# Cross attention of a post-norm decoder: scores as three rounded products, a looked-up weight table decoded in 32 units instead of 64

## The chip, the cores and the metric
One core of a Trainium2 chip runs one program. The metric is the device time of one execution in microseconds. Engines are named as in the profile: PE (TensorE) with PEld (its weight loads), DVE (VectorE), ACT (ScalarE), POOL (GpSimd) and SP (SyncE, which issues most DMAs here). All times below are in us unless marked ns.

## The reference
Six stages on x (4 chunks of 512 rows, width 512), each followed by a residual sum and a layer norm: two attentions and a feed-forward of layer 0, then self attention, cross attention and feed-forward of layer 1. The change touches the cross attention and the decoding of the last feed-forward's weights:

```python
q = (hidden_states @ Wq).reshape(B, Sq, 16, 128)
k = (encoder_hidden_states @ Wk).reshape(B, Skv, 16, 128)
v = (encoder_hidden_states @ Wv).reshape(B, Skv, 16, 128)
q = rmsnorm(q, gq)
k = rmsnorm(k, gk)
scores = jnp.einsum('bqhd,bkhd->bhqk', q, k) * scale
attn = jax.nn.softmax(scores, axis=-1)
out = jnp.einsum('bhqk,bkhd->bqhd', attn, v).reshape(B, Sq, 2048) @ Wo
# next stage: three weight matrices, each w = lut[idx] with 16 table entries, 3 * 512 * 1376 indices
```

## The kernel before
**Stages.** Each stage loops over the 4 chunks c. The cross attention (stage 3 of the code, line 820 on) is written out by hand for PE, ACT, DVE, POOL and SP; every engine runs its own list, tied by semaphores. A chunk has a start (keys and values of the first four heads, x turned), 16 heads hh in four groups g of four, an output phase (16 heads against Wo) and the norms.

**PE in head hh** (lines 934 to 947): scores(hh), four tiles of 128 x 512, each a full f32 product of q4 and kr (line 905, shown as L594); queries(hh+1), 12 rounded products of 512 columns (L844); weighted(hh-1), full f32 (L594); in the second head of a group the values of the next group, 24 rounded products (L844); turn_keys(hh+1) (L890); query_squares(hh+1) (L897); turn_weights(hh) (L912); in the third head the keys of the next group, 24 rounded products. A rounded product works on fp32r operands: a number is split into its rounded part (hi, written by ACT) and the rest (lo, a subtraction on DVE), and hi*hi + hi*lo + lo*hi makes the product. queries, keys and values are made so before the change already.

**Banks.** Tiles of the list TILES4 go through three PSUM banks in turn (bank4, line 835): a tile waits until ACT has copied the tile three places before it. A query tile is followed by the output tile of head hh-1, then by value tiles or the turned keys, then by the turned weights. The scores have banks 4 to 7.

**DVE in head hh** (lines 1730 to 1758): for each of four tiles the maximum (L1734) and its scaled negative (L1738, which for the first tile waits for POOL's power of the query's mean square); then four reciprocals (L1743) and scalings (L1745) after ACT's exponentials; in the last head of a group key_scale (L1686), on which turn_keys of the next head waits; look_up(c, hh); query_mean(hh+1) (L1692); in the third head key_norms (L1675, L1677). In chunk 0 it also makes the rests of the weights (L1696, L1700, L1704), in head 12 that of the next chunk's context (L1708).

**look_up** (line 1628) decodes one of 64 units of 128 x 258 indices, one a head: four masks of index bits (L1634, L1636), eight entries of the table's pairs (L1640), seven predicated choices in three rounds of 4, 2 and 1 (L1648), each round behind one wait. All work of one unit stands together, after the softmax of its head. SP loads the indices and stores the 64 results; stage 4 reads them.

**ACT in head hh**: exponentials (L1240), squares (L1230) and copy of the next query (L1040 through bring), the copies of the output tile, of values, turned keys (turned_keys, line 1233), turned weights and keys.

**Output phase** (line 955): in chunks 0 to 2 each head takes 12 rounded products (L960 to L962). ACT rounds the head's output and its slice of Wo (round_out), DVE makes both rests (out_rest, L1717 and L1718), two buffers each; PE waits for out_rest(hh), ACT for PE to be done with head hh-2. DVE does nothing else there. The last chunk's output phase is in full f32 (L970).

## Time and profile before

| what | us |
|---|---|
| three runs | 2951.90, 2947.09, 2952.43; median 2951.9 |
| the profiled execution | 2950.78, its span 2948.8 |
| PE busy / DVE busy / ACT busy / POOL busy | 2639.7 / 2067.5 / 1178.3 / 641.9 |
| mean granted TensorE clock | 0.95 |
| cross attention, first scores of chunk 0 to first scores of chunks 1, 2, 3 | at 1262.7, 1610.3, 1928.4, 2247.7 |

The profile is one execution. Busy time is that of an engine's own instructions; matmuls overlap, so a row of several has the span of all. A number in brackets is the engine's idle time just before the instruction, and what ended it. The granted clock is the share of 2.4 GHz that TensorE was given: 1.00, or 0.50, which is 1.2 GHz.

### The profile page before, as it was taken

The numbers are of one execution on the slowest core, as the hardware profiler recorded it, in microseconds if no ns is written. First come the engines' busy times: TensorE is split into PE (matmuls) and PEld (weight loads), VectorE is DVE, ScalarE is ACT, GpSimd is POOL, SyncE is SP. The second block draws the span as 40 slices with busy tenths as digits, with TensorE's granted clock in tenths as the row PEclk, the third lists the DMA queues.
The fourth block names the chain that finished last, engine by engine and source line by source line (L and its number), as shares of the span: only waits on it lengthen the run. The fifth ranks groups of instructions, "written<-read, shape, count | busy, mean of one in ns | idle before, by whom it ended". The sixth has DMA issues, their size and how long they took to land.

```text
span 2948.8 us, 30680 instructions
## 1 busy us (share of the span) xinstructions
PE 2639.7 (90%) x9586; PEld 1640.0 (56%) x9586; DVE 2067.5 (70%) x4063; ACT 1178.3 (40%) x2139; POOL 641.9 (22%) x569
## 2 busy tenths in 40 slices
PE   6888888888869978789989999999989998999998
PEld 2333333333337844456657666666666665488886
DVE  3996996996996547778876888588867887322232
ACT  4335325326333312255554555355544555121111
POOL 0642543534520135411101111011101110000000
PEclk9998988988979999999999999999999999999999
DMA  3111111111220212233233222332222223400000
GB/s 120 57 50 44 65 43 55 61 50 51 69 109 29 79 43 86 77 122 101 86 102 116 83 83 76 92 108 83 83 74 95 83 72 107 138 1 29 29 15 14
DMA packets 90792, 212.58 MB, mean 72 GB/s; under 512 B 9987, under 2 KB 34819, under 8 KB 86534
## 3 DMA queue, kind: packets, MB, share of 16 engines
q1 hardware_dynamic: 81510, 178.51, 18.7%
q0 software_dynamic: 5472, 21.01, 1.9%
q10 hardware_dynamic: 3648, 11.08, 1.0%
q8 instruction: 80, 1.31, 0.2%
q14 instruction: 82, 0.67, 0.1%
HBM read 164.10 MB, written 46.47 MB: 71 GB/s over the span
## 4 chain that ended last, share of the span: by engine, by line
PE 59%; DVE 20%; issue 11%; POOL 5%; ACT 3%; DMA 1%; SPq 1%; DVEq 0%; POOLq 0%; ACTq 0%
PE bank L594 21%; PE bank L844 8%; PE bank L912 3%; DVE h L1441 3%; PE bank L984 3%; PE bank L985 3%; PE bank L988 3%; POOL h L1822 3%; DVE val L1640 2%; DVE sm L1734 2%; DVE val L1648 2%; PE bank L714 2%; PE bank L970 2%; PE bank L960 2%; PE bank L961 1%
## 5 line engine op out<-in xcount | busy, mean ns | idle before, releaser
L1822 POOL TENSOR_TENSOR h<-du,Bb 128x1024 f32<-128x1024 f32 x128 | 306.2, 2394 | 188.1 <-DVE h L1446 172.2
L1441 DVE TENSOR_TENSOR_SCAN h<-bank,h 128x512 f32<-128x512 f32 x256 | 297.8, 1203 | 22.4 <-POOL h L1822 15.1
L1095 ACT ACTIVATE bank<-dt,A 128x512 f32<-128x512 f32 x256 | 175.9, 691 | 327.7 <-DVE h L1441 327.6
L1240 ACT ACTIVATE p<-bank,sm,rq 128x512 f32<-128x512 f32 x256 | 199.1, 778 | 244.5 <-DVE sm L1738 244.5
L1890 POOL TENSOR_TENSOR rq<-rq,mhalf 128x4 f32<-128x4 f32 x64 | 69.4, 1084 | 798.3 <-DVE rq L1692 798.3
L594 PE MATMUL bank<-pT,v 128*128 128x512 f32 x512 | 236.7, 606 | 2.7 <-ACT pT L1040 2.7
L211 POOL TENSOR_SCALAR rstd<-mv 128x1 f32<-128x1 f32 x96 | 25.2, 263 | 956.5 <-DVE mv L205 956.5
L594 PE MATMUL bank<-kr,q 128*128 128x512 f32 x512 | 233.0, 598 | 0.0
L714 PE MATMUL bank<-h,ident 128*128 128x512 f32 x256 | 153.2, 682 | 84.6 <-DVE h L1446 84.5
L844 PE MATMUL bank<-x_hi,wxq_s 128*128 128x512 f32 x512 | 190.8, 454 | 6.5 <-DVE x_lo L1713 6.5
L1648 DVE COPY_PREDICATED val<-msk,val 128x258 f32<-128x258 int32 x448 | 173.6, 449 | 27.8 <-DVE val L1648 0.2
L1734 DVE TENSOR_REDUCE sm<-bank 128x1 f32<-128x512 f32 x256 | 175.2, 684 | 23.6 <-PE bank L594 23.6
L1777 DVE TENSOR_TENSOR h<-bank,sg 128x512 f32<-128x512 f32 (+1 forms) x44 | 30.4, 690 | 228.5 <-PE bank L988 228.5
L1446 DVE TENSOR_TENSOR h<-h,Cb 128x1024 f32<-128x1024 f32 x128 | 173.8, 1358 | 6.6
L1640 DVE TENSOR_SCALAR val<-msk,lx,le 128x258 uint32<-128x258 uint32 x512 | 171.7, 409 | 7.2 <-DVE msk L1636 0.5
L594 PEld LDWEIGHTS bank<-pT,v 128*128 128x128 f32 x512 | 99.1, 194 | 106.9 <-issue 97.6
L912 PE MATMUL bank<-ident,p 128*128 128x128 f32 x1024 | 138.9, 293 | 17.4 <-DVE p L1745 16.2
L1040 ACT ACTIVATE pT<-bank 128x512 f32<-128x512 f32 x256 | 134.7, 603 | 46.9 <-PE bank L912 46.8
L594 PEld LDWEIGHTS bank<-kr,q 128*128 128x128 f32 x512 | 94.4, 193 | 94.4 <-issue 93.4
L715 PE MATMUL bank<-h,ident 128*128 128x512 f32 x256 | 140.9, 634 | 0.0
L714 PEld LDWEIGHTS bank<-h,ident 128*128 128x128 f32 x256 | 43.6, 202 | 172.3 <-DVE h L1446 137.3
L912 PEld LDWEIGHTS bank<-ident,p 128*128 128x128 f32 x1024 | 125.6, 155 | 24.4 <-DVE p L1745 19.5
(228 smaller groups left out, 5686.4 us busy)
## 6 DMA issues: line engine op xcount, KB each, us to landing
wxq_s<-wq_dram SPq DMA_DIRECT2D x48, 512.0 KB, 4.5
Bb<-bc_dram SPq DMA_DIRECT2D x32, 512.0 KB, 3.6
Cb<-bc_dram SPq DMA_DIRECT2D x32, 512.0 KB, 3.7
x_dram<-xo POOLq DMA_DIRECT2D x16, 1024.0 KB, 4.7
xc<-x_dram SPq DMA_DIRECT2D x16, 1024.0 KB, 5.2
woh<-in_Wo SPq DMA_DIRECT2D x64, 256.0 KB, 2.7
wxv_s<-wkv_dram SPq DMA_DIRECT2D x12, 1024.0 KB, 5.3
wxk_s<-wkv_dram SPq DMA_DIRECT2D x12, 1024.0 KB, 7.4
```

The costliest lines, as they stand in the source:

```text
L594: m = pe.matmul(dst, l, r, start=(k == 0), stop=(k == len(pairs) - 1))
L714: pe.matmul(bank[4 + et][:, :], ident[:, :], h[:, U % HR, 0, :], start=(w == 0), stop=False)
L844: m = pe.matmul(dst, l, r, start=(n == 0), stop=(n == len(pairs) - 1))
L912: m = pe.transpose(d[:, t * P:(t + 1) * P], p4[:, t, k * P:(k + 1) * P], ident[:, :])
L1095: act.activation(bank[2 + n][:, :], dt[:, et, :], ACT.Exp, scale=A[:, et, 2 * w + n:2 * w + n + 1]).then_inc(dA_ready, 1)
L1240: act.activation(p4[:, t, :], bank[4 + t][:, :], ACT.Exp, bias=sm4[:, 4 + t:5 + t], scale=rq[:, hh % 2, 1, t:t + 1], accum_out=sm4[:, 8 + ...
L1441: dve.tensor_tensor_scan(h[:, s, n, :], bank[2 + n][:, :], h[:, s, n, :], 0.0, ALU.mult, ALU.add).then_inc(scanned, 1)
L1446: dve.tensor_tensor(h[:, s, :, :], h[:, s, :, :], Cb[:, w % 2, :, :], ALU.mult).then_inc(hC_ready, 1)
L1640: dve.tensor_scalar(val[:, j, :].bitcast(U32), msk[:, 0, :].bitcast(U32), lx[:, j:j + 1], le[:, j:j + 1], ALU.bitwise_and, ALU.bitwise_xor ...
L1648: dve.copy_predicated(val[:, s, :], msk[:, b, :], val[:, s + (1 << (b - 1)), :]).then_inc(lut_step, 1)
L1734: dve.tensor_reduce(sm4[:, t:t + 1], bank[4 + t][:, :], AX.X, ALU.max).then_inc(max_ready, 1)
L1822: pool.tensor_tensor(h[:, U % HR, :, :], du[:, et:et + 1, :].to_broadcast([P, 2, S]), Bb[:, w % 2, :, :], ALU.mult).then_inc(dBu_ready, 1)
```

## The change
Scores are made of q_hi, q_lo, k_hi and k_lo. ACT's copy of the query writes q_hi (fp32r) and DVE subtracts it from the bank (q_rest), so the bank is now also held until q_rest; ACT copies the turned keys to kr as before, then rounds kr to k_hi, and DVE makes k_lo (k_rest). q4 and kr had two buffers; q_hi, q_lo, k_hi, k_lo and kr have one.

The table has 32 units of 516 columns. A unit is cut into masks and four pairs, which stand in different heads; each choice waits for the instruction before it. The number of units per group of heads is LUTS; what a chunk has left of its 8 units (2, 1, 1, 0) is decoded in its output phase. In a group with two units head 0 holds masks and pairs 1 and 2 of the first, head 1 its pairs 3 and 4 and masks and pair 1 of the second, head 2 pairs 2 and 3, head 3 pair 4. Index buffers and results alternate between two places, and SP's loads and stores move with the units.

```diff
-UNITS = B * XH
+UNITS = B * XH // 2
+UB = UNITS // B
+LUTS = ((2, 1, 2, 1), (2, 2, 2, 1), (2, 2, 2, 1), (2, 2, 2, 2))
...
-        w_hi3 = Space(nc, s4.at)("w_hi3", [P, 2, D], F32R); q4 = s4("q4", [P, 2, S])
+        w_hi3 = Space(nc, s4.at)("w_hi3", [P, 2, D], F32R); q_hi = s4("q_hi", [P, S], F32R); q_lo = s4("q_lo", [P, S], F32R)
...
-        w_lo3 = Space(nc, s4.at)("w_lo3", [P, 2, D], F32R); kr = s4("kr", [P, 2, S])
+        w_lo3 = Space(nc, s4.at)("w_lo3", [P, 2, D], F32R); k_hi = s4("k_hi", [P, S], F32R); k_lo = s4("k_lo", [P, S], F32R)
+        kr = s4("kr", [P, S])
...
-        idx = s4("idx", [P, UL], I32); msk = s4("msk", [P, 4, UL], I32); val = s4("val", [P, 8, UL])
+        idx = s4("idx", [P, 2, UL], I32); msk = s4("msk", [P, 3, UL], I32); val = s4("val", [P, 5, UL])
@@ SP @@
+                def load_idx(n):
+                    if n >= 2:
+                        sp.wait_ge(lut_step, START + 19 * (n - 1))
+                    sp.dma_start(idx[:, n % 2, :], io["idx"][bass.ds(n, 1), :, :].rearrange("a p n -> p (a n)")).then_inc(idx_in[n % 2], 16)
+                def store_unit(n):
+                    sp.wait_ge(lut_step, START + 19 * (n + 1))
+                    sp.dma_start(w_dram.rearrange("(u p n) -> u p n", p=P, n=UL)[bass.ds(n, 1), :, :]
+                                 .rearrange("a p n -> p (a n)"), val[:, 4 * (n % 2), :]).then_inc(w_out[n % 2], 16)
...
+                            g, n = hh // 4, UB * c + sum(LUTS[c][:hh // 4])
+                            if hh % 4 == 0:
+                                load_idx(n)
+                                if g and LUTS[c][g - 1] == 2:
+                                    store_unit(n - 1)
+                                if LUTS[c][g] == 2:
+                                    load_idx(n + 1)
+                            if hh % 4 == 2:
+                                store_unit(n)
@@ PE @@
                             pe.wait_ge(a_done, START + A0[3] + after(c, PER_A[3], max(0, k - 2)))
+                            for hh in range(XH):
+                                if TILES4["q", hh] == k - 3:
+                                    pe.wait_ge(q_split, START + after(c, XH, hh + 1))
...
-                            ready4("kT", hh)
+                            pe.wait_ge(q_split, START + after(c, XH, hh + 1))
+                            pe.wait_ge(k_split, START + after(c, XH, hh + 1))
...
-                                group(bank[4 + t][:, :], [(q4[:, hh % 2, t * P:(t + 1) * P], kr[:, hh % 2, :])], v_full)
+                                tt = slice(t * P, (t + 1) * P)
+                                three4(bank[4 + t][:, :], [(q_hi[:, tt], k_hi[:, :]), (q_hi[:, tt], k_lo[:, :]), (q_lo[:, tt], k_hi[:, :])], v_full)
@@ ACT @@
-                            bring(q4[:, hh % 2, :], d)
+                            bring(q_hi[:, :], d)
...
-                            bring(kr[:, hh % 2, :], got("kT", hh), scale=g2[:, 2:3])
+                            act.wait_ge(k_split, START + after(c, XH, hh))
+                            bring(kr[:, :], got("kT", hh), scale=g2[:, 2:3])
+                            act.wait_ge(a_done, START + A0[3] + after(c, PER_A[3], TILES4["kT", hh] + 1))
+                            act.activation(k_hi[:, :], kr[:, :], ACT.Copy).then_inc(k_rounded, 1)
@@ DVE @@
+                def masks(n):
+                    r = n % 2
+                    dve.wait_ge(idx_in[r], START + 16 * (n // 2 + 1))
+                    dve.wait_ge(lut_step, START + 19 * n)
+                    dve.tensor_scalar(msk[:, 0, :], idx[:, r, :], 31, 31, ALU.logical_shift_left, ALU.arith_shift_right).then_inc(lut_step, 1)
+                    for b in (1, 2):
+                        dve.tensor_scalar(msk[:, b, :], idx[:, r, :], 1 << b, None, ALU.bitwise_and).then_inc(lut_step, 1)
+                    dve.wait_ge(lut_step, START + 19 * n + 3)
+                    dve.tensor_scalar(idx[:, r, :], idx[:, r, :], 8, None, ALU.bitwise_and).then_inc(lut_step, 1)
+                def entry(j, s):
+                    dve.tensor_scalar(val[:, s, :].bitcast(U32), msk[:, 0, :].bitcast(U32), lx[:, j:j + 1], le[:, j:j + 1],
+                                      ALU.bitwise_and, ALU.bitwise_xor).then_inc(lut_step, 1)
+                def choose(s, m, other, n, done):
+                    dve.wait_ge(lut_step, START + 19 * n + done)
+                    hold(dve)
+                    dve.copy_predicated(val[:, s, :], m, val[:, other, :]).then_inc(lut_step, 1)
+                def first_pair(n):
+                    s = 4 * (n % 2)
+                    dve.wait_ge(w_out[n % 2], START + 16 * (n // 2))
+                    dve.wait_ge(lut_step, START + 19 * n + 4)
+                    entry(0, s)
+                    entry(1, 1)
+                    choose(s, msk[:, 1, :], 1, n, 6)
+                def second_pair(n):
+                    s = 4 * (n % 2)
+                    entry(2, 2)
+                    entry(3, 3)
+                    choose(2, msk[:, 1, :], 3, n, 9)
+                    choose(s, msk[:, 2, :], 2, n, 10)
+                def third_pair(n):
+                    dve.wait_ge(lut_step, START + 19 * n + 11)
+                    entry(4, 1)
+                    entry(5, 2)
+                    choose(1, msk[:, 1, :], 2, n, 13)
+                def fourth_pair(n):
+                    s = 4 * (n % 2)
+                    dve.wait_ge(lut_step, START + 19 * n + 14)
+                    entry(6, 2)
+                    entry(7, 3)
+                    choose(2, msk[:, 1, :], 3, n, 16)
+                    choose(1, msk[:, 2, :], 2, n, 17)
+                    choose(s, idx[:, n % 2, :], 1, n, 18)
...
+                        def q_rest(hh):
+                            dve.wait_ge(a_done, START + A0[3] + after(c, PER_A[3], TILES4["q", hh] + 1))
+                            dve.tensor_tensor(q_lo[:, :], bank[TILES4["q", hh] % 3][:, :], q_hi[:, :], ALU.subtract).then_inc(q_split, 1)
+                        def k_rest(hh):
+                            dve.wait_ge(k_rounded, START + after(c, XH, hh + 1))
+                            dve.tensor_tensor(k_lo[:, :], kr[:, :], k_hi[:, :], ALU.subtract).then_inc(k_split, 1)
@@ DVE, at a chunk's start, ahead of query_mean(0) @@
+                        q_rest(0)
+                        k_rest(0)
@@ DVE, after the softmax of head hh @@
+                            if hh + 1 < XH:
+                                q_rest(hh + 1)
                             if c == 0 and hh + 2 < XH:
                                 wxq_rest(hh + 2)
                             if hh % 4 == 3 and hh < XH - 1:
                                 key_scale(hh // 4 + 1)
-                            look_up(c, hh)
+                            if hh % 4 == 0:
+                                masks(n)
+                            if hh % 4 == 1:
+                                third_pair(n)
+                                fourth_pair(n)
+                            if hh % 4 == 2 and two:
+                                second_pair(n + 1)
+                            if hh + 1 < XH:
+                                k_rest(hh + 1)
+                            if hh % 4 == 0:
+                                first_pair(n)
+                                second_pair(n)
+                            if hh % 4 == 1 and two:
+                                masks(n + 1)
+                                first_pair(n + 1)
+                            if hh % 4 == 2 and two:
+                                third_pair(n + 1)
+                            if hh % 4 == 3 and two:
+                                fourth_pair(n + 1)
@@ DVE, output phase of chunks 0 to 2 @@
                             for hh in range(XH):
                                 out_rest(hh)
+                                if hh == 1:
+                                    masks(n)
+                                if hh == 3:
+                                    first_pair(n)
+                                if hh == 4:
+                                    second_pair(n)
+                                if hh == 6:
+                                    third_pair(n)
+                                if hh == 7:
+                                    fourth_pair(n)
@@ the same for unit n + 1 of chunk 0 behind heads 9, 10, 12, 13 and 15 @@
```

In the diff, two = the group has two units. In SP's list of the output phase the indices of the units left are loaded behind load_wo(1), and their results stored ahead of load_wo(11) (chunk 0's first) and behind the last load_wo.

## Rows read from the trace of the kernel before

**Rows 1.** The page, shares of the chain that ended last, by engine.

```profile
PE 59%; DVE 20%; issue 11%; POOL 5%; ACT 3%; DMA 1%; SPq 1%; DVEq 0%; POOLq 0%; ACTq 0%
```

**Rows 2.** Window, chunk 1, heads 0-14: length, busy by engine, clock, DMA.

```profile
1611.42:1841.00 229.58, 225.62 (x985) 150.74 (x984) 198.51 (x581) 127.59 (x264) 27.70 (x33) 1.00 0.29 89
```

**Rows 3.** Chain of waits, chunk 1, in order: start, us, what.

```profile
1671.02 3.44 PE bank L594 x8
...
1677.25 3.43 PE bank L594 x8
1681.12 0.79 PE bank L897 x8
...
1683.75 3.44 PE bank L594 x8
...
1701.93 3.44 PE bank L594 x8
...
1733.96 3.44 PE bank L594 x8
```

**Rows 4.** Timeline of DVE, chunk 1, head 5: start, us, line, what.

```profile
1687.64 0.68 DVE L1734 TENSOR_REDUCE sm<-bank 128x1 f32<-128x512 f32 x1
...
1694.13 0.29 DVE L1634 TENSOR_SCALAR msk<-idx 128x258 int32<-128x258 int32 x1
1694.33 0.69 DVE L1636 TENSOR_SCALAR msk<-idx 128x258 int32<-128x258 int32 x3
1695.13 2.68 DVE L1640 TENSOR_SCALAR val<-msk,lx,le 128x258 uint32<-128x258 uint32 x8
1697.96 3.02 DVE L1648 COPY_PREDICATED val<-msk,val 128x258 f32<-128x258 int32 x7
```

**Rows 5.** Timeline of DVE, chunk 1, head 7.

```profile
1722.51 0.68 DVE L1734 TENSOR_REDUCE sm<-bank 128x1 f32<-128x512 f32 x1
...
1728.14 2.49 DVE L1686 TENSOR_TENSOR kt<-kt,kss 128x512 f32<-128x512 f32 x4
```

**Rows 6.** Timeline of DVE, start of chunk 2.

```profile
1918.82 1.88 DVE L1713 TENSOR_TENSOR x_lo<-bank,x_hi 128x512 fp32r<-128x512 f32 x3
```

**Rows 7.** Groups of DVE by form: count, busy us, mean ns, idle.

```profile
L1648 DVE COPY_PREDICATED val<-msk,val 128x258 f32<-128x258 int32 x448 | 173.6, 449 | 27.8 <-DVE val L1648 0.2
L1640 DVE TENSOR_SCALAR val<-msk,lx,le 128x258 uint32<-128x258 uint32 x512 | 171.7, 409 | 7.2 <-DVE msk L1636 0.5
...
L1423 DVE TENSOR_SCALAR h<-yacc 128x512 f32<-128x512 f32 x16 | 6.7, 421 | 29.9 <-ACT yacc L1085 29.9
```

**Rows 8.** Timeline of DVE, narrow window: fourth and fifth choice of a unit.

```profile
2031.50 1.05 DVE L1648 COPY_PREDICATED val<-msk,val 128x258 f32<-128x258 int32 x2
```

**Rows 9.** Groups of ACT by form, one of them.

```profile
L1270 ACT ACTIVATE o_hi<-oT 128x512 fp32r<-128x512 f32 x48 | 30.3, 631 | 78.1 <-DMA woh<-in_Wo 60.1 <-PE bank L962 9.6 <-issue 8.4
```

**Rows 10.** Timeline of PE, chunk 1, from the scores of head 13 on.

```profile
1809.46 3.60 PE L594 MATMUL bank<-kr,q 128*128 128x512 f32 x8
...
1823.27 3.60 PE L594 MATMUL bank<-kr,q 128*128 128x512 f32 x8
...
1836.55 3.60 PE L594 MATMUL bank<-kr,q 128*128 128x512 f32 x8
...
1847.60 3.68 PE L912 MATMUL bank<-ident,p 128*128 128x128 f32 x16 [4.02 <-DVE p L1745]
...
1858.67 0.50 PE L960 MATMUL bank<-w_hi,o_hi 128*128 128x512 f32 x1 [0.69 <-ACT oT L1040]
```

**Rows 11.** Timeline of PE, chunk 0, end of head 3.

```profile
1326.11 1.11 PE L890 MATMUL bank<-ident,kt 128*128 128x128 f32 x4 [5.09 <-DVE kt L1686]
```

**Rows 12.** Timeline of DVE, output phase of chunk 0.

```profile
1548.70 0.69 DVE L1717 TENSOR_TENSOR o_lo<-oT,o_hi 128x512 fp32r<-128x512 f32 x1 [1.50 <-ACT w_hi L1271]
```

**Rows 13.** Timeline of PE, chunk 0, head 13; then a window just after.

```profile
1503.31 1.05 PE L897 MATMUL bank<-ones,sq 128*128 128x1 f32 x8 [2.46 <-ACT q L1040]
...
1505.20:1508.40 3.20, 3.20 (x11) 2.33 (x10) 3.09 (x11) 1.98 (x4) 0.00 (x0) 0.50 0.00 0
```

More of the change, by code:

```diff
@@ L353, in build @@
         ctx_rounded = sem("ctx_rounded"); ctx_split = sem("ctx_split"); x3_split = sem("x3_split")
+        q_split = sem("q_split"); k_rounded = sem("k_rounded"); k_split = sem("k_split")
         o_rounded = sem("o_rounded"); o_split = sem("o_split")
@@ L545, in _ @@
                         for hh in range(XH):
-                            sp.wait_ge(lut_step, START + after(c, 19 * XH, 19 * hh))
-                            sp.dma_start(idx[:, :], io["idx"][bass.ds(c * XH + hh, 1), :, :].rearrange("a p n -> p (a n)"))\
-                                .then_inc(idx_in, 16)
-                            if hh:
-                                store_unit(c, hh - 1)
+                            g, n = hh // 4, UB * c + sum(LUTS[c][:hh // 4])
[7 more added lines that the diff above has]
+                                store_unit(n)
                             if c == 0:
@@ L576, in _ @@
                             load_chunk(4, 0, 0, rows_of)
+                        n = UB * c + sum(LUTS[c])
                         for hh in range(2):
                             load_wo(c, hh)
-                        sp.wait_ge(lut_step, START + after(c, 19 * XH, 19 * XH))
-                        store_unit(c, XH - 1)
+                        if LUTS[c][3] == 2:
+                            store_unit(n - 1)
+                        for m in range(n, UB * (c + 1)):
+                            load_idx(m)
                         for hh in range(2, XH):
+                            if hh == 11 and n + 1 < UB * (c + 1):
+                                store_unit(n)
                             load_wo(c, hh)
+                        if n < UB * (c + 1):
+                            store_unit(UB * (c + 1) - 1)
             if stages >= 5:
@@ L1317, in _ @@
                 act.wait_ge(a_done, START + A0[4])
-                act.wait_ge(w_out, START + 16 * UNITS)
+                for n in range(2):
+                    act.wait_ge(w_out[n], START + 16 * UNITS // 2)
                 act.wait_ge(p_ready, START + B * 4 * XH)
@@ L1745, in _ @@
                                 dve.tensor_scalar(p4[:, t, :], p4[:, t, :], sm4[:, 12 + t:13 + t], None, ALU.mult).then_inc(p_ready, 1)
+                            g, n, two = hh // 4, UB * c + sum(LUTS[c][:hh // 4]), LUTS[c][hh // 4] == 2
+                            if hh + 1 < XH:
+                                q_rest(hh + 1)
                             if c == 0 and hh + 2 < XH:
@@ L1761, in _ @@
                         if c < B - 1:
+                            n, late = UB * c + sum(LUTS[c]), UB - sum(LUTS[c])
                             for hh in range(XH):
                                 out_rest(hh)
+                                if hh == 1:
[8 more added lines that the diff above has]
+                                    fourth_pair(n)
+                                if hh == 9 and late == 2:
+                                    masks(n + 1)
+                                if hh == 10 and late == 2:
+                                    first_pair(n + 1)
+                                if hh == 12 and late == 2:
+                                    second_pair(n + 1)
+                                if hh == 13 and late == 2:
+                                    third_pair(n + 1)
+                                if hh == 15 and late == 2:
+                                    fourth_pair(n + 1)
                         if c == B - 1 and stages >= 5:
```

27 lines of the change are left out of this document (2 added, 25 removed).

## Prediction
> **What bounds the kernel now.** The chain of the whole run is 59% TensorE and 20% VectorE [rows 1]. The window over heads 0 to 14 of chunk 1 says more: TensorE is busy 225.62 of 229.58 us at full clock, VectorE 198.51 [rows 2]. So from chunk 1 on a head lasts as long as its matrix work, and VectorE has little room. The chain in order of time gives one group of four heads piece by piece [rows 3]: scores (S) 3.44, queries (Q) 2.79 for 12 rounded products (1677.25 less the scores' end), weighted values (W) 3.43, turning keys (KT) 0.44, squares 0.79 and turning weights 1.84. A plain head is 12.73, the one with the next values 18.18, and the group takes 1733.96 - 1671.02 = 62.94. The VectorE timeline tells how close the second engine is [rows 4, 5]: softmax 6.49 (5.63 in a head that follows key norms, where the query mean was early), then a table unit: masks 1.00, entries 2.83, choices 2.9, together 6.73. That is 13.2 in a head of 12.73.
>
> **PE's side of the change.** Twelve rounded products cost 2.79, so S falls from 3.44 to 2.80, 0.64 a head, 41 us in 64 heads if nothing else became late. From the start of S, Q now ends at 5.6, W at 9.0, KT at 9.5, the weights are turned between 10.3 and 12.1.
>
> **VectorE's side.** A rounded difference of 512 columns follows its neighbour by 0.60 (1.88 for three, 0.68 of it one) [rows 6]: q_rest and k_rest add 1.2 a head, 77 us. A unit of 516 columns: an operation with no scalar takes 0.42 at 512 columns and 0.29 at 258 (three masks in 0.69 are 0.20 apart) [rows 4, 7], so masks are 0.34 apart, and 1.53 with the wait ahead of the fourth. An entry is 0.409 long, eight are 0.324 apart; the same slope of 0.134 makes 0.54 and 0.46. A choice is 0.449; seven in 3.02 with two that wait for their predecessor, 0.60 after it [rows 4, 8], leave 0.34 between free ones. At one column a cycle (the 0.60 of 512 columns less a fixed 0.07) 258 more columns add 0.27: 0.72 long, 0.61 apart, 0.86 where it waits. Entry to waiting choice is 0.68. Every choice now waits, so first pair = 0.46+0.68+0.61 = 1.76, second 2.62, third 1.76, fourth 3.47; with the masks 11.1 a unit against 13.4 for two old ones. 32 units save 74 us, the differences cost 77: VectorE's work does not shrink, four units (44 us) only leave the heads. Bounds for a unit: 9.1 if waits cost nothing (three between choices at 0.25, four behind entries at 0.22 and two behind masks at 0.19 are 2.0 less), 12.2 if entries run one column a cycle (eight at 0.13 more). I take 11.1, whose parts lie nearest to rows.
>
> On that price a rule speaks otherwise. The Trainium skill (VectorE: DVE Perf Modes, The DRAIN you can't avoid) reports that a semaphore after each of eight copies costs nothing extra; by it a unit is 9.1. The row with 0.60 between waiting choices against 0.34 disagrees, and I go by the row.
>
> **A group with two units, chunks 1 to 3**, in us from the start of each S. VectorE enters the first head at 3.2 (found by going once round). ScalarE rounds the keys after copying them, 0.63 like any 512 columns [rows 9], so k_rest can't start before KT's end + 1.7, and S of the next head waits for it. Behind ScalarE's new wait and rounding stand the copies of the turned weights, 0.6 later; their own transposes end no earlier, so I count nothing. Behind TensorE's new wait for the query's rest stand, in second heads, three value tiles and all that follows, in the others the turned weights, which wait for the softmax just before it anyway.
> First head: softmax to 9.7, q_rest 10.3, masks 11.8, k_rest 12.4, keys split 12.6: S starts at 12.6 (12.73 before). First and second pair put VectorE 4.3 into the next head.
> Second: softmax to 10.8, the query's rest is ready at 11.5. The values' second tile reuses the query's bank and wanted it at 10.4: 1.1 idle. Third and fourth pair to 16.8, k_rest waits for the rounded keys until 17.8; S at 18.7 (18.18 before). Masks and first pair: lag 3.2.
> Third: q_rest at 10.3, second pair, k_rest, third pair to 15.3, all beside the 5.6 of the keys. S at 17.85; key norms leave a lag of 3.0.
> Fourth: softmax to 8.6, q_rest 9.2, and only then key_scale (2.49 for four [rows 5]), ready at 11.8 where turning wanted it at 9.0: 2.8 idle. S at 14.9; third and fourth head are 32.7 together (32.03 before). Fourth pair: lag 3.2, closed.
> Sum 64.0 against 62.9: **+1.1 a group, 9 groups, +10**. What S gives is lost in the second and fourth head.
>
> **The last four heads.** No values or keys are made here. In head 13 third and fourth pair (5.4) stand ahead of k_rest, and VectorE is already 5.4 late (context rest and two pairs): 5.4+6.3+0.6+5.4+0.6+0.15 = 18.5, where it was 1823.27 - 1809.46 = 13.8 [rows 10]. Head 14 then is 12.1 (13.3). Head 15 gains: TensorE waits 4.02 for a late softmax, and 22.1 pass to the output phase [rows 10]. With no unit before it, turning starts at 6.7 after S; 1.8, a copy 0.7, 3.43 and a copy 0.7 make 13.4: -8.7. Heads 12 to 15 of chunks 1 and 2: +3.3 - 8.7 = -5.4 each; chunk 0 by the same steps -6.6; chunk 3, whose second unit fills heads 13 to 15, +0.2. Together **-17**.
>
> **Chunk 0.** VectorE also takes the weights' rests, and turning the first keys of a group idles 5.09 [rows 11]. In its group 1, with one unit, I get an idle of 2.7, in groups 0 and 2, with two, 4.0. With the steps above, the weights' rests added, the one with one unit gets 4.7 shorter, the two others 1.6 and 1.5: **-8**. Bounds: -14 if all of the old idle goes and -3 if the later pairs eat it.
>
> **Output phase.** A head needs 2.8 of TensorE, and VectorE is free 1.5 between two rests [rows 12]. Pairs longer than that push: 0.2+1.05+0.2+1.9 = 3.35 a unit; masks are free. Four units, the last pair of chunk 0 after head 15 delaying the norms 2.3 in place of 1.9: **+14**. Cover gone: rests of heads 4, 5, 7 and 8 come late, and the queue of W loads with them. The index loads and stores move on SP's queue; each is waited for with 5 us to spare but one store ahead of a load in chunk 0's head 11, bounds 0 and 1 us, taken as 0.
>
> **Chunk starts.** Rounding and resting the first keys lies open, 0.63+0.68 less what squares cover: +1.1 (bounds 0 and 1.4) four times, **+4**.
>
> **Clock.** After an idle of 2.46 the granted clock was 0.50 for 3.2 us [rows 13], half of 2.4 GHz; after 4.02 the 16 transposes took 3.68 [rows 10], against 1.84 in the chain. The new idles of 2.8 (9 times) and 4.2 (head 13, four times) should do the same: 1.7 of which the lag absorbs half, taken 1.0; and 3 (1.6 to 5). **+21**, bounds 5 and 35. The Trainium skill (TensorE: Matmul & The Clock Gate, Why this matters for your kernels) names a longer gap than 2.8 before throughput drops; by it the nine would cost nothing and the sum is 9 lower. The row at 2.46 speaks against it.
>
> **Sum.** +10-17-8+14+4+21 = +24. The profiled execution took 2950.8 (span 2948.8 and 2.0 around), so 2975, 0.8% slower; the median is 1.1 above that execution, within the 5 us spread of three runs. I forecast 2975, own range 2960 to 2992.
>
> **Rivals.**
> A, faster: VectorE's unit fits. If an operation that waits starts as early as a free one, a unit is 9.1. The lag in each second head falls by 2, its idle goes, head 13 is 1.5 shorter, the output overrun halves: groups 61.6 (-1.3, 9 times, -12), last heads -23, chunk 0 -12, output +6, starts +4, clock +12: 2926. For it: slopes beyond 258 columns of a choice are not in the trace. Against: the 0.60. The skill's rule above is this mechanism. Chance 0.25.
> B, slower still: entries at one column a cycle. Two scalars already make an entry 0.12 longer than a mask; if the slope is 0.27, a unit costs 1.1 more, 32 times on VectorE's path, most of it passed on: +30, 3005. For it: nothing wide with two raw scalars in the rows. Chance 0.12.
> C, no change: the sum stands but the clock stays at 1.00 through the idles of 2.8 and costs 3 in all after head 13: 2957. Chance 0.13.
> The change might not do what it says only if three products cost what the full one did; the 12 in 2.79 exclude that. The forecast has 0.50.
> The faster side opens where second, third and fourth heads together stay under their old 50.2: in the sum it is 51.4, so 1.2 a group decides between A and the rest.
>
> **How the numbers follow.** A measurement here can tell about 0.2%, 6 us. Faster: A and the low edge of C, 0.27; same: most of C, 0.13; slower: forecast and B, 0.60. The range 2930 to 3000 leaves out parts of A and B.
>
> **What would show it.** In the changed profile: 12 score products in 2.8; waiting choices 0.86 apart; a first tensor reduction 4.3 after S in second heads; idle ahead of the keys' turning 2.8 in fourth heads; S to S 18.5 in head 13 and 13.4 from head 15 to the output; four longer heads a unit in the output phases; half clock after these idles. I am wrong if group periods fall below 62, or if VectorE waits for TensorE's scores in most heads.

## The result and the profile after

| | us |
|---|---|
| four runs after | 2983.92 to 2987.59; median 2985.24 |
| four runs before beside them | 2947.09 to 2952.43; median 2952.10 |
| ratio | 1.0117, 95% interval 1.01 to 1.0135 |
| the profiled execution's span | 2982.2 (before 2948.8) |

The changed kernel is 1.2% slower. The forecast of 2975 had the sign right and was 10 too low; its range and its own narrower range (2960 to 2992) hold the result. The page of the changed kernel, busy time by engine:

```profile
PE 2627.0 (88%) x9842; PEld 1709.9 (57%) x9842; DVE 2074.3 (70%) x3583; ACT 1216.0 (41%) x2203; POOL 646.7 (22%) x569
```

TensorE has 12.7 less to do (before 2639.7), VectorE 6.8 more, ScalarE 37.7 more, and the kernel takes 33 longer: the added time is idle TensorE and TensorE at half clock. The window over heads 0 to 14 of chunk 1, and two narrower ones behind the turning of the keys, one in chunk 3 and one in chunk 1 (columns as in [rows 2]):

```profile
1614.54:1852.47 237.93, 221.62 (x1036) 167.96 (x1037) 196.56 (x458) 135.63 (x278) 29.91 (x34) 0.96 0.27 89
...
2327.80:2331.00 3.20, 3.01 (x27) 2.92 (x28) 0.98 (x3) 2.20 (x5) 0.00 (x0) 1.00 0.03 5
1672.90:1676.80 3.90, 3.88 (x27) 3.88 (x28) 1.61 (x3) 2.79 (x5) 0.00 (x0) 0.76 0.00 0
```

Against [rows 2], TensorE's busy time fell by 4.0 and its idle time rose from 3.96 to 16.31. VectorE's busy time is 2 lower: it is not short of time over the chunk, it is late at certain points. The chunk's granted clock is 0.96 where it was 1.00.

TensorE's timeline of chunk 1 names the points. Head 1 of the chunk, then head 3, then heads 13 to 15:

```profile
1636.00 0.69 PE L868 MATMUL bank<-wxv_s,ctx_hi 128*128 128x512 f32 x2 [1.06 <-DVE q_lo L1759]
...
1672.92 0.66 PE L914 MATMUL bank<-ident,kt 128*128 128x128 f32 x4 [2.61 <-DVE kt L1749]
...
1674.22 3.00 PE L938 MATMUL bank<-ident,p 128*128 128x128 f32 x16
...
1831.30 1.31 PE L921 MATMUL bank<-ones,sq 128*128 128x1 f32 x8 [1.62 <-ACT q_hi L1066]
1832.49 3.33 PE L938 MATMUL bank<-ident,p 128*128 128x128 f32 x16
1838.86 0.77 PE L868 MATMUL bank<-k_hi,q_hi 128*128 128x512 f32 x1 [3.04 <-issue]
...
1862.04 3.70 PE L615 MATMUL bank<-pT,v 128*128 128x512 f32 x8 [0.81 <-ACT pT L1066]
1866.42 0.50 PE L986 MATMUL bank<-w_hi,o_hi 128*128 128x512 f32 x1 [0.69 <-ACT oT L1066]
```

These are the waits of the forecast: the second value tile behind the query's rest (1.06 in the chunk's first group, 0.92 and 0.93 in the others; forecast 1.1), turning the keys behind key_scale (2.61; 2.8), the scores of head 14 (3.04, put down to issue; VectorE's timeline has the keys' rest end just then), and head 15, whose late softmax [rows 10] is gone.

VectorE in heads 5 and 6 of chunk 1, from the fourth pair of a unit on:

```profile
1702.88 1.01 DVE L1671 TENSOR_SCALAR val<-msk,lx,le 128x516 uint32<-128x516 uint32 x2
1704.04 1.66 DVE L1678 COPY_PREDICATED val<-msk,val 128x516 f32<-128x516 int32 x2
1705.84 0.75 DVE L1678 COPY_PREDICATED val<-idx,val 128x516 f32<-128x516 int32 x1
1707.47 0.69 DVE L1763 TENSOR_TENSOR k_lo<-kr,k_hi 128x512 fp32r<-128x512 f32 x1 [0.88 <-ACT k_hi L1264]
1708.08 0.42 DVE L1663 TENSOR_SCALAR msk<-idx 128x516 int32<-128x516 int32 x1
...
1709.76 1.01 DVE L1671 TENSOR_SCALAR val<-msk,lx,le 128x516 uint32<-128x516 uint32 x2
1710.91 0.74 DVE L1678 COPY_PREDICATED val<-msk,val 128x516 f32<-128x516 int32 x1
1711.54 0.15 DVE L1755 TENSOR_SCALAR rq<-bank 128x4 f32<-128x4 f32 x1
...
1718.70 1.00 DVE L1671 TENSOR_SCALAR val<-msk,lx,le 128x516 uint32<-128x516 uint32 x2
1719.85 1.65 DVE L1678 COPY_PREDICATED val<-msk,val 128x516 f32<-128x516 int32 x2
1721.38 0.68 DVE L1763 TENSOR_TENSOR k_lo<-kr,k_hi 128x512 fp32r<-128x512 f32 x1
1721.97 1.00 DVE L1671 TENSOR_SCALAR val<-msk,lx,le 128x516 uint32<-128x516 uint32 x2
1723.12 0.75 DVE L1678 COPY_PREDICATED val<-msk,val 128x516 f32<-128x516 int32 x1
1723.77 0.15 DVE L1755 TENSOR_SCALAR rq<-bank 128x4 f32<-128x4 f32 x1
```

By differences of starts: masks 1.68, first pair 1.78, second 2.68, third 1.80, fourth 3.59 where what follows needn't wait (output phase of chunk 0, shown below): 11.5 a unit, forecast 11.1. The fourth pair above takes 3.71 to the end of its last choice. Two waiting choices are 1.65 - 0.75 = 0.90 apart (0.86).

**Stretches.** From the starts of the scores in both timelines, after less before:

| stretch | forecast | measured |
|---|---|---|
| heads 0 to 11 of chunks 1, 2, 3 (9 groups), clock with it | +10 +9 | +22.7 |
| heads 12 to 15, four chunks, clock with it | -17 +12 | -6.5 |
| heads 0 to 11 of chunk 0 | -8 | +2.0 |
| output phases of chunks 0 to 2, with 2.6 of chunk 0's norms | +14 | +10.9 |
| starts of chunks 1 to 3 (that of chunk 0 is in the row "stages ahead") | +4 for four | +3.2 |
| f32 output phase of chunk 3 | 0 | +3.9 |
| stages ahead and behind | 0 | -2.8 |
| sum | +24 | +33.4 |

### The profile page after: what moved, and what is told of

It reads as the page before. It is cut to its first block and busy times, and to the rows that moved or that the text cites. A ratio compares the mean times of both kernels' runs of the same rounds, so it can differ in the third digit from the quotient of the medians.

```text
span 2982.2 us, 30701 instructions
## 1 busy us (share of the span) xinstructions
PE 2627.0 (88%) x9842; PEld 1709.9 (57%) x9842; DVE 2074.3 (70%) x3583; ACT 1216.0 (41%) x2203; POOL 646.7 (22%) x569
## 5 line engine op out<-in xcount | busy, mean ns | idle before, releaser
L615 PE MATMUL bank<-pT,v 128*128 128x512 f32 x512 | 230.5, 593 | 3.2 <-ACT pT L1066 3.2
L868 PE MATMUL bank<-x_hi,wxq_s 128*128 128x512 f32 x512 | 164.4, 403 | 6.5 <-DVE x_lo L1784 6.5
L1678 DVE COPY_PREDICATED val<-msk,val 128x516 f32<-128x516 int32 x192 | 144.4, 752 | 29.2 <-DVE val L1671 2.0
L938 PE MATMUL bank<-ident,p 128*128 128x128 f32 x1024 | 149.4, 305 | 8.0 <-DVE p L1818 2.7
L938 PEld LDWEIGHTS bank<-ident,p 128*128 128x128 f32 x1024 | 132.4, 161 | 17.8 <-DVE p L1818 6.0
L1818 DVE TENSOR_SCALAR p<-p,sm 128x512 f32<-128x512 f32 x256 | 124.5, 486 | 9.1
L1671 DVE TENSOR_SCALAR val<-msk,lx,le 128x516 uint32<-128x516 uint32 x256 | 128.4, 545 | 2.0
L868 PE MATMUL bank<-k_hi,q_hi 128*128 128x512 f32 x256 | 111.5, 436 | 18.4 <-issue 18.3
```

The source lines that it names most:

```text
L615: m = pe.matmul(dst, l, r, start=(k == 0), stop=(k == len(pairs) - 1))
L868: m = pe.matmul(dst, l, r, start=(n == 0), stop=(n == len(pairs) - 1))
L938: m = pe.transpose(d[:, t * P:(t + 1) * P], p4[:, t, k * P:(k + 1) * P], ident[:, :])
L1671: dve.tensor_scalar(val[:, s, :].bitcast(U32), msk[:, 0, :].bitcast(U32), lx[:, j:j + 1], le[:, j:j + 1], ALU.bitwise_and, ALU.bitwise_xor ...
L1818: dve.tensor_scalar(p4[:, t, :], p4[:, t, :], sm4[:, 12 + t:13 + t], None, ALU.mult).then_inc(p_ready, 1)
```

## The experiments

Periods of a head are from the start of its scores to those of the next. "Second" and "fourth" head are those of a group of four. A time in brackets after a kernel's time is the range of its runs.

**The two halves apart.** First the products alone: the kernel before with the new scores, its 64 units of 258 columns left as they were.

```diff
+ q_rest(hh + 1)                       # behind the softmax
- look_up(c, hh)
+ look_up(c, hh, rest_of_keys)         # k_rest between entries and choices,
+                                      # in second heads behind the unit
```

> The change's products alone: scores as three rounded products, with q_rest, k_rest and ScalarE's rounding, but the table as before, 64 units of 258 columns, one a head (k_rest stands between the entries and the choices of the unit, in second heads behind it). Theory (VectorE's order and load decide, the products only give TensorE time back that it then waits): a plain head costs VectorE 6.5 + 1.2 + 6.7 + 0.1 = 14.5 where TensorE needs 12.1, so plain heads take 14.5 instead of 12.7 and a group some 4 more than before: 3010 to 3025. Rival (the parts of the table are what costs): without them the 41 us of TensorE time come through, 2915 to 2950.

2997.4 (2996.9 to 3006.7), ratio 1.0165 (1.0146 to 1.0184): slower by 46, less than expected, and far from the rival. The expected place was wrong in part: of the first heads of a group, which were to take 14.5, those of the later groups of chunks 1 to 3 take 12.8 to 14.2. The nine groups are 31.0 longer, and 25.0 of it is in the fourth heads, 15.5 to 17.0 long for 13.65: key_scale stands behind the query's rest, TensorE idles 2.08 ahead of turning the keys where it idled 0.71, and its transposes run slower behind it in eight of the nine. TensorE's timeline, head 7 of chunk 1:

```profile
1741.58 0.65 PE L895 MATMUL bank<-ident,kt 128*128 128x128 f32 x4 [2.08 <-DVE kt L1697]
```

In three of the nine second heads the rest of the keys costs something too. In VectorE's timeline, head 5 of chunk 1, VectorE still waits 1.45 behind a whole unit for ScalarE's rounded keys, and the scores start once k_rest is done.

```profile
1711.68 0.69 DVE L1711 TENSOR_TENSOR k_lo<-kr,k_hi 128x512 fp32r<-128x512 f32 x1 [1.45 <-ACT k_hi L1245]
```

Then the table alone: the changed kernel with q4, kr and the scores of before.

```diff
- three4(..., [(q_hi, k_hi), (q_hi, k_lo), (q_lo, k_hi)])
+ group(..., [(q4[:, hh % 2, tt], kr[:, hh % 2, :])])
- q_rest(hh + 1); k_rest(hh + 1)
```

> The change's table alone: 32 units in parts as in the changed kernel, scores in full f32 as before, no rests of queries and keys. Theory: heads stay on TensorE's 12.7, groups of chunks 1 to 3 near 62.9, the late softmax of head 15 goes (8 less in each of the chunks), chunk 0 loses half of its idle ahead of turning keys, the output phases keep some 10 more: 2905 to 2925, faster than both kernels. Rival (wide units with a wait ahead of each choice are what costs): 2960 or more.

2930.1 (2926.0 to 2934.5), ratio 0.9926 (0.9913 to 0.9939), 5 above the band. Window over heads 0 to 14 of chunk 1:

```profile
1608.33:1832.93 224.60, 221.66 (x979) 149.34 (x978) 180.29 (x429) 127.63 (x263) 29.62 (x35) 1.00 0.29 96
```

The groups take what they took before (the nine together 559.2, before 559.4): TensorE sets them, and the 18 that VectorE has less to do there buy nothing. The gain is 31.9 in heads 12 to 15, where head 15 no longer has a unit in front of the output phase; the output phases give back 9.5. So the halves are worth +46 and -21. Their sum of +24 is less than the +33 of both together, but the first places its rests otherwise, so this difference isn't a clean reading of how they collide.

**Single waits of the changed kernel.** The rest of the keys ahead of the fourth pair in head 13:

```diff
  third_pair(n)
+ if hh == 13: k_rest(hh + 1)
  fourth_pair(n)
```

> The changed kernel with k_rest(14) ahead of the fourth pair in head 13, nothing else. Theory: head 13 goes from 18.8 to 14.8 in chunks 0 to 2 and head 14 gets shorter by the half clock that follows the idle, 1; chunk 3 about even: 15 less, 2970. Rival (the idle there is hidden or moves on to the next head): within 4 of the changed kernel, 2981 to 2989.

2971.8 (2971.0 to 2976.9), ratio 1.0074 (1.006 to 1.0088), as expected. TensorE's timeline, head 13 of chunk 1:

```profile
1831.99 1.38 PE L921 MATMUL bank<-ones,sq 128*128 128x1 f32 x8 [1.63 <-ACT q_hi L1066]
1833.23 3.27 PE L938 MATMUL bank<-ident,p 128*128 128x128 f32 x16
1836.26 0.48 PE L868 MATMUL bank<-k_hi,q_hi 128*128 128x512 f32 x1
```

The idle of 3.04 ahead of head 14's scores is gone, head 13 takes 15.55 (18.84), and head 14 12.08 (13.61) as its scores run at full clock. In chunk 3 the wait only moves, as expected: head 13 is 3.7 shorter and head 14 3.3 longer. The place and the price of this term are shown.

key_scale ahead of the rests:

```diff
+ if hh % 4 == 3: key_scale(hh // 4 + 1)
  q_rest(hh + 1)
  if c == 0: wxq_rest(hh + 2)
- if hh % 4 == 3: key_scale(hh // 4 + 1)
```

> The changed kernel with key_scale ahead of q_rest in fourth heads, nothing else. Theory: the idle ahead of turning keys falls from 2.6 to 2.0 in twelve groups, 7 less, and up to 11 more if the half clock after it goes too: 2967 to 2978. Rival (q_rest's wait then stands on the path instead, or the clock falls anyway and the rest of the group absorbs it): 2982 to 2987.

2969.9 (2962.8 to 2972.1), ratio 1.0059 (1.0046 to 1.0073). Inside the band, but the gain sits elsewhere than in chunks 1 to 3: they give 5.8, chunk 0 gives 16.7. VectorE's timeline of the changed kernel, chunk 0, head 7, tells why:

```profile
1391.36 0.68 DVE L1759 TENSOR_TENSOR q_lo<-bank,q_hi 128x512 fp32r<-128x512 f32 x1
1393.69 0.69 DVE L1767 TENSOR_TENSOR wxq_s<-wxq,wxq_s 128x512 fp32r<-128x512 f32 x1 [1.64 <-ACT wxq_s L1277]
1394.30 2.49 DVE L1749 TENSOR_TENSOR kt<-kt,kss 128x512 f32<-128x512 f32 x4
```

and the same head with key_scale first:

```profile
1391.24 2.49 DVE L1749 TENSOR_TENSOR kt<-kt,kss 128x512 f32<-128x512 f32 x4
1393.65 0.68 DVE L1759 TENSOR_TENSOR q_lo<-bank,q_hi 128x512 fp32r<-128x512 f32 x1
1394.25 0.68 DVE L1767 TENSOR_TENSOR wxq_s<-wxq,wxq_s 128x512 fp32r<-128x512 f32 x1
```

In chunk 0, VectorE waits 1.64 for ScalarE's rounded query weights, with key_scale queued behind. With key_scale first that wait is covered, TensorE idles 1.41 in place of 4.34, and the head takes 13.62 in place of 19.24. Heads 3 and 11 of the chunk take 14.33 and 16.22 in place of 19.25 and 19.16. The kernel before has this wait too (it idles 5.09 there), so the 16.7 are not a cost of the change but a gain on top of it.

The weighted values ahead of the queries in second heads, so that the query's bank is wanted again later:

```diff
+ if first: weighted(hh - 1)           # first = hh in 1, 5, 9
  queries(hh + 1)
- if hh: weighted(hh - 1)
+ if hh and not first: weighted(hh - 1)
```

> The changed kernel with the weighted values ahead of the queries in the second heads of groups 0 to 2 (tile list, TensorE and ScalarE alike), so that the third value tile, not the second, reuses the query's bank, 1.4 later. Theory: the idle of 1.06 inside the values (2.1 in chunk 0) goes or falls below 0.8, some 13 less in all: 2968 to 2976. Rival (VectorE's lateness shows up in the next wait, so the idle only moves): 2981 to 2989.

2972.6 (2966.3 to 2979.7), ratio 1.0065 (1.0048 to 1.0082). The idle of 1.06 is gone and second heads of chunk 1 take 17.70 to 17.84 (18.76 to 18.89).

All three together:

> The three reorderings together: k_rest(14) ahead of the fourth pair in head 13, key_scale ahead of q_rest in fourth heads, weighted values ahead of queries in second heads. Theory (each wait stands by itself): 13 + 15 + 13 less than the changed kernel, 2940 to 2950, faster than the kernel before. Rival (they share one cause, VectorE's load, and the gains overlap): 2955 to 2970.

2937.2 (2923.6 to 2939.5), ratio 0.9941 (0.9919 to 0.9962), a little under the band. They are worth 48 together and 13.5, 15.3 and 12.6 apart, 41 in sum. In the profiles 17.7 of it is in heads 0 to 11 of chunk 0, most of it the wait that the kernel before has too; 16.2 is in the nine groups, which had lost 22.7, and 15.0 in heads 12 to 15. So the waits that the change made hold about as much as it cost, and the rest comes from an older one.

**The output phase.** The same kernel with a unit in seven pieces behind seven heads; then the table alone with the same pieces.

```diff
- hh 1: masks; hh 3, 4, 6, 7: pairs 1 to 4
+ hh 1: masks; hh 2: pair 1; hh 3, 4: pair 2; hh 5: pair 3; hh 6, 7: pair 4
```

> The kernel of the three reorderings, with the output phase's unit in seven pieces behind seven heads, none over 1.8 (masks; first pair; entries 2 and 3 with a choice; a choice; third pair; entries 6 and 7 with a choice; two choices). Theory: the pushes of 1.0 and 1.9 a unit become 0.2 each and chunk 0 ends its phase without a pair behind head 15: some 10 less than without it, 2930 to 2940. Rival (the phase is as long for another reason, the loads of Wo): within 3 of the kernel with the three reorderings alone.

> The table alone (scores in full f32) with the output phase's units in the same seven pieces. Theory: 2930 less some 10, 2916 to 2924, the fastest of all. Rival as for the spread with the three reorderings: 2927 or more.

2930.2 (2915.4 to 2938.2), ratio 0.9925 (0.9899 to 0.9951), and 2923.0 (2919.6 to 2927.1), ratio 0.9899 (0.9883 to 0.9916). Both are 7 below their kernels without it, as expected, though each pair of intervals overlaps a little. The profiles show the place: the three output phases lose 8.0 in the first and 6.3 in the second. VectorE's timeline of the changed kernel, output phase of chunk 0, shows what was in the way, the whole fourth pair ahead of a head's rests:

```profile
1558.76 1.00 DVE L1671 TENSOR_SCALAR val<-msk,lx,le 128x516 uint32<-128x516 uint32 x2
1559.90 1.66 DVE L1678 COPY_PREDICATED val<-msk,val 128x516 f32<-128x516 int32 x2
1561.71 0.74 DVE L1678 COPY_PREDICATED val<-idx,val 128x516 f32<-128x516 int32 x1
1562.35 0.68 DVE L1788 TENSOR_TENSOR o_lo<-oT,o_hi 128x512 fp32r<-128x512 f32 x1
```

At this point the version without the three products was ahead of the one with them by 7, within overlapping intervals.

**Are the products worth their order, with VectorE free?** Both kernels with the table's operations cut to two columns, so the decoded weights are left out:

```diff
- dve.copy_predicated(val[:, s, :], m, val[:, other, :])
+ dve.copy_predicated(val[:, s, 0:2], m[:, 0:2], val[:, other, 0:2])
```

> The changed kernel with every operation of the table cut to 2 columns (same instructions, waits, loads and stores; the five result buffers are filled with zeros once), so the table's result is left out and VectorE has room. Theory (VectorE's load and order take back what the products give): heads fall to TensorE's 12.1, second heads to 17.6, fourth heads keep an idle near 2 because the last copy of the new keys, norms and scaling stand behind it; groups of chunks 1 to 3 near 61.6, last heads 12.1: 2875 to 2895. It should be 15 to 25 below the kernel before with the same cut. Rival (three rounded products with two more splits don't pay even so): not below it.

> The kernel before with every operation of the table cut to 2 columns (result buffers filled with zeros once), the table's result left out. Theory: groups of chunks 1 to 3 stay at 62.9, since TensorE bounds them; the late softmax of head 15 and part of chunk 0's idle go: 2900 to 2912. Rival (VectorE bounds the old heads too): groups fall below 62, total below 2890.

The kernel before so cut took 2908.1 (2907.0 to 2909.7), as expected. The changed one took 2923.1 (2910.4 to 2927.8): 15 above it, where 15 to 25 below was expected. A miss, and the run that taught most. Its timeline of TensorE, chunk 1, head 7, and then its clock there:

```profile
1717.26 1.04 PE L915 MATMUL bank<-ident,kt 128*128 128x128 f32 x4 [2.00 <-DVE kt L1754]
...
1719.66 3.65 PE L939 MATMUL bank<-ident,p 128*128 128x128 f32 x16
```

```profile
1717.20:1722.90 5.70, 5.64 (x28) 5.64 (x29) 1.69 (x8) 2.92 (x5) 0.91 (x1) 0.52 0.05 17
```

With hardly a table, TensorE still idles 2.00 for key_scale, and everything up to the next scores runs near half clock (transposes 3.65, against 2.02 when the clock stays). A fourth head takes 16.6 to 16.9, in the cut kernel before mostly 13.66. Over the nine groups that is +17.6, while heads 12 to 15 are 4.0 shorter. So the volume of the table isn't what makes the products dear: the chain softmax, query's rest, key_scale does, 5.6, 0.6 and 2.5 in a row from the first maximum at 2.36 on.

The cut kernel with the three changes of order:

> The kernel after with the three changes of order (rest of the keys ahead of the fourth pair in head 13, key scaling ahead of the query's rest, weighted values ahead of the queries in second heads), and with the table's operations cut to 2 of 516 columns, so the decoded weights are left out. The same cut without the changes of order took 2923, with the scores of before 2908. Theory: what the three products lose there stands in the fourth heads, where the query's rest (0.60) goes ahead of the key scaling, TensorE idles 2.0 ahead of turning the keys, and runs at half clock for 5 us behind it: 16.7 to 16.9 a fourth head against 13.66 with the scores of before. With the scaling first the idle is 1.4 and the clock should stay at 1.00: fourth heads 13.5, nine of them 3.2 shorter (-29), chunk 0's three (idle 4.3 now) 4 shorter each (-12): 2876 to 2890, and the products are worth 20 to 30 when VectorE has nothing else to do. Rival: the order is not it, the longer way of the keys (copy, rounding, rest) costs it in any order, and the time stays at 2905 or above. Half way (idle 1.4 but still half clock): 2900.

2874.2 (2873.4 to 2884.3), ratio 0.9744 (0.9725 to 0.9763): 34 below the cut kernel before, 49 below the same without the new order. The theory stands as to the order, and the rival falls. The 34 aren't the worth of the products, though: 19.5 of it is in heads 0 to 11 of chunk 0, where the cut kernel before also idles 4.34 with its key_scale behind the query weights' wait, and its order was left as it was. The nine groups give 13.6 and heads 12 to 15 7.6. Two of the three changes had nothing to do here (second heads 17.53 against 17.55, head 13 12.08 against 12.27); the gain is that of key_scale first. Fourth heads of chunk 1, heads 3 and 7:

```profile
1628.34 0.66 PE L918 MATMUL bank<-ident,kt 128*128 128x128 f32 x4 [1.41 <-DVE kt L1763]
...
1629.64 2.02 PE L942 MATMUL bank<-ident,p 128*128 128x128 f32 x16
...
1689.37 0.66 PE L918 MATMUL bank<-ident,kt 128*128 128x128 f32 x4 [1.40 <-DVE kt L1763]
...
1690.78 3.50 PE L942 MATMUL bank<-ident,p 128*128 128x128 f32 x16
```

The same idle, once with the clock kept and once without: 13.61 and 15.19 for the head.

**A version that beats both.** key_scale goes further ahead, between the maxima and the reciprocals of the softmax, in the kernel with the three changes and the spread output phase.

```diff
  for t in range(NT): ...              # maxima
+ if hh % 4 == 3: key_scale(hh // 4 + 1)
  for t in range(NT): ...              # reciprocals, scalings
- if hh % 4 == 3: key_scale(hh // 4 + 1)
```

> The kernel after with the three changes of order and the output phase's units spread over its heads (2930), and with the four key scalings moved further ahead: between the maxima and the reciprocals of the softmax in heads 3, 7 and 11. Theory: turning the keys then finds them scaled and its idle of 2.0 goes (ready at about 8.7 after S, wanted at 9.1); the four scaled weights come 2.5 later and turning them waits 0.8 in its place; the half clock behind an idle of 2.0, seen in some of the fourth heads, is not seen behind 0.8. Fourth heads 13.0 to 13.4 in place of 14.2 and 15.7: 12 heads by 1.2 to 2: 2906 to 2916, below the kernel with the scores of before in the same form (2923). Rival: what is taken from the keys' idle is given to that of the weights, one for one, and the time stays at 2925 to 2935.

2903.2 (2902.8 to 2909.0), ratio 0.9837 (0.9824 to 0.9851): 1.6% faster than the kernel before, a little under the band, and 20 below the table alone with the spread output phase, the best one without three products. TensorE's timeline, chunk 1, head 7:

```profile
1702.99 0.60 PE L917 MATMUL bank<-ident,kt 128*128 128x128 f32 x4
1703.43 0.95 PE L924 MATMUL bank<-ones,sq 128*128 128x1 f32 x8
1705.84 1.98 PE L941 MATMUL bank<-ident,p 128*128 128x128 f32 x16 [1.46 <-DVE q_lo L1768]
```

The keys' idle is gone, the turned weights wait 1.46 for the query's rest (0.8 was expected), and none of the twelve fourth heads loses the clock: 13.50 to 13.90, in chunk 0 12.95. The nine groups take 551.5 (before 559.4, after 582.1).

The 20 don't show that the products pay. Against the table alone with the spread output phase, the profiles have heads 0 to 11 of chunk 0 at -19.0, the nine groups at -7.6 and heads 12 to 15 at +8.3. The first is in the fourth heads, 12.95 in place of 20, and there the version without three products has the same wait ahead of key_scale. Its VectorE timeline, chunk 0, head 7:

```profile
1394.39 0.69 DVE L1749 TENSOR_TENSOR wxq_s<-wxq,wxq_s 128x512 fp32r<-128x512 f32 x1 [2.91 <-ACT wxq_s L1267]
1395.00 2.49 DVE L1739 TENSOR_TENSOR kt<-kt,kss 128x512 f32<-128x512 f32 x4
```

key_scale ahead of that wait would start 3.5 earlier there; by an estimate from these rows and the fourth heads of 13.66 in its other chunks, this version would gain 10 to 19 as well. It wasn't run, so which of the two is the faster in the best order of each stays open.

## Why the prediction was right, and where it was off

**Right, with its mechanism.** The forecast's case was that VectorE's work doesn't shrink and that what the scores give is lost in waits of second and fourth heads. Heads of 12.6, 18.7, 17.85 and 14.9 were worked out for a group with two units. Measured in the later groups of chunks 1 to 3: 12.1 to 12.8, 18.8 to 18.9, 18.0, and 14.78 where the clock stayed. Head 13 is 18.84 (18.5), head 15 up to the output phase 13.95 (13.4). The first maximum of second heads comes 4.2 to 4.4 after the scores (4.3), and twelve score products take 2.8. With the three waits taken away the nine groups lose 16.2 of their 22.7 and heads 12 to 15 15.0, which shows that these waits are the cost; and the table alone shows that the halved table by itself is a gain of 0.7%.

**The unit.** 11.5 where 11.1 was forecast; an entry is 0.545 long (0.54), a choice 0.752 (0.72). Rival A, a unit of 9.1 by waits that cost nothing, is out: waiting choices are 0.90 apart, and what need not wait starts 0.63 to 0.65 behind a choice (1710.91 and 1723.12 above). The Trainium skill (VectorE: DVE Perf Modes, The DRAIN you can't avoid) reports that a semaphore set behind each copy costs nothing extra. The trace doesn't contradict that, since the choices that the prediction has 0.34 apart [rows 4] set one too. It shows that the figure is no price of a wait, as rival A used it: a wait for the choice before, with the one semaphore instruction that the kernel puts behind it (hold), costs 0.25. No run parts the two. Rival B, entries at one column a cycle, is out too: 0.13 more for 258 columns.

**The clock.** +21 was forecast in all. In the nine fourth heads of chunks 1 to 3 the idle of 2.6 left the clock at 1.00 twice and halved it seven times; their mean is 16.10 against 14.78, so 1.3 each and 12 together (forecast 1.0 and 9). The groups cost 12.7 more than the +10 of the sum without the clock, and the clock is most of that. Rival C, a clock that stays through these idles, is out. The gap that the Trainium skill names (TensorE: Matmul & The Clock Gate, Why this matters for your kernels) is longer than the 2.00 behind which the cut kernel lost its clock nine times in nine, so the trace disagrees with it.

**Wrong: the chunk 0 term.** It said "In its group 1, with one unit, I get an idle of 2.7, in groups 0 and 2, with two, 4.0", and -8 with bounds -14 and -3. The idle is 4.34 in all three, and the groups are 2.0 longer. The step that failed counted VectorE's late start, which did go (its first maximum came 5.51 after the scores in head 7, now 2.36), as gained. It left out that VectorE waits for ScalarE in wxq_rest. The same head's row of the kernel before:

```profile
1396.31 0.69 DVE L1696 TENSOR_TENSOR wxq_s<-wxq,wxq_s 128x512 fp32r<-128x512 f32 x1 [0.54 <-ACT wxq_s L1248]
```

The wait was 0.54 and is 1.64 now: 1.10 of it, the query's rest of 0.60 and the scores' 0.64, by which TensorE comes earlier, leave 0.8 of the 3.15, and a fourth head is 1.6 shorter. The idle is 4.34 as well in the table alone and in both cut kernels, whatever VectorE has to do there, which fits a wait for ScalarE; it is longer only in the kernel before (5.09) and in the products alone (5.7). The second heads (0.4 to 2.1 longer, 2.1 of idle ahead of the values' second tile) and the third heads of groups with two units (2.2 longer) take more than that back. The run with key_scale first shows the first part, since it takes the wait out of the way and chunk 0 gives 16.7.

**Sizes.** The output phases came to +10.9 for +14: the heads behind the second and the fourth pair are 3.89 and 4.76 long against 2.9, which is 2.85 a unit for 3.35. The kernel before has two long heads there itself, 3.94 and 4.29 in chunks 1 and 2, which make the difference some 2.4 smaller. Two stretches had no term: the f32 output phase of chunk 3, +3.9, and the stages ahead, -2.9. Neither is explained. Over all the kernels of this study, whose code is the same in these stages but for the start of chunk 0, the time up to the first scores was 1252.9 to 1265.3 and that output phase 62.7 to 70.3, so they are no cost of the change that one profile can show.

**Left open.** What the kernel without three products would take with key_scale moved ahead, and so what the products are worth by themselves; why an idle of one length halves the clock in one head and not in the next; and whether the rests of the query could go ahead of the softmax's scalings as key_scale did, which wasn't tried.

## What to carry to other kernels

Work moved from the bounding engine to a second one isn't paid by totals: VectorE had 30% of the run free, and each rest cost where it stood in its engine's order. Before judging such a change, list for the second engine what the first waits for next, and put that ahead of work with slack; here moving four instructions in twelve heads took the version with three products from 7 behind the one without them to 20 ahead. Before crediting the change with such a gain, give the kernel that it is compared with the same order: here most of the 20 stands in chunk 0, where both had the wait and only one was rid of it. When the lateness of an engine goes away, ask what it had hidden, as the rounded weights here.

## What the runs showed of the hardware

- **Half clock behind short idles.** Counted by the 16 transposes of the weights behind the idle, which take 2.0 at full clock and 2.8 to 3.7 where it fell. Idles of 0.71 to 0.73 ahead of turning the keys never cost the clock in chunks 1 to 3 of the kernel before and of the one with the table alone (18 heads). Behind the one idle of 1.06 (cut kernel before, head 3 of chunk 1) the granted clock was 0.65 over the next 4.7. Behind 1.40 it was halved in 4 of 12 heads of the cut kernel with three changes. Behind about 2.0 it was halved in 4 of 9 in the kernels with key_scale first and with all three changes, in 5 of 9 with the spread output phase, in 8 of 9 in the products alone and in 9 of 9 in the cut changed kernel. Behind 2.6 it was halved in 7 of 9 in the changed kernel, in 9 of 9 with only head 13 changed and in 6 of 9 with only the second heads changed. The 1.46 of the last kernel, which stands one step later, ahead of turning the weights, cost it in none of 9. A lost clock costs 0.9 to 2.7 more than the idle.
- **Predicated choices are dearer by the column than entries.** 258 to 516 columns: 449 to 752 ns for a choice, 409 to 545 ns for an entry with two scalars, from the groups by form:

```profile
L1678 DVE COPY_PREDICATED val<-msk,val 128x516 f32<-128x516 int32 x192 | 144.4, 752 | 29.2 <-DVE val L1671 2.0 <-DVE val L1678 0.2
L1671 DVE TENSOR_SCALAR val<-msk,lx,le 128x516 uint32<-128x516 uint32 x256 | 128.4, 545 | 2.0
```
